# Five small constant TensorE products behind each piece of the state sums in a selective scan

## Time and profile before

| | us |
|---|---|
| median of 3 runs (5586.12 to 5604.31) | 5591.09 |
| profiled execution, its own time | 5583.17 |
| its span | 5581.4 |
| TensorE busy (products) | 4171.4 (75%) |
| VectorE busy | 3825.9 (69%) |
| ScalarE busy | 2731.3 (49%) |
| GpSimd busy | 1705.0 (31%) |

### The profile page before, as it was taken

How to read it: one execution, slowest core, us unless ns; L and a number is a source line. 1 busy time by engine, 2 the same in 40 slices (tenths; PEclk the granted TensorE clock), 3 DMA queues, 4 the chain that set the end, 5 groups by cost and what they waited for, 6 DMA issues and landing times. The chain is left out here.

```text
span 5581.4 us, 75326 instructions
## 1 busy us (share of the span) xinstructions
PE 4171.4 (75%) x23106; PEld 1512.8 (27%) x23106; DVE 3825.9 (69%) x5339; ACT 2731.3 (49%) x3579; POOL 1705.0 (31%) x938
## 2 busy tenths in 40 slices
PE   5587874632888886542787876676999999999994
PEld 3344441210111112210121112351333333333331
DVE  4355554455888884455789895556877877787783
ACT  1354550554444443465444444142666666666661
POOL 0000000144999991044799994000000000000000
PEclk8798996655667767755567678765999999999997
DMA  3311113123222222032222222132111111111114
GB/s 107 91 22 25 27 26 58 43 87 91 63 53 67 55 51 56 24 91 79 65 65 57 62 53 70 36 129 82 40 40 40 40 40 43 55 41 40 40 40 82
DMA packets 140635, 317.91 MB, mean 57 GB/s; under 512 B 27882, under 2 KB 86115, under 8 KB 135694
## 3 DMA queue, kind: packets, MB, share of 16 engines
q1 hardware_dynamic: 140238, 312.83, 20.9%
HBM read 204.28 MB, written 108.01 MB: 56 GB/s over the span
## 5 line engine op out<-in xcount | busy, mean ns | idle before, releaser
L1818 DVE TENSOR_REDUCE l3a_mx<-l3a_mx 128x1 f32<-128x384 f32 x2719 | 1326.0, 551 | 353.1 <-PE l3a_mx L1694 344.4
L1799 ACT ACTIVATE l3a_p<-l3a_s 128x1024 f32<-128x1024 f32 (+1 forms) x1080 | 978.4, 937 | 427.7 <-PE l3a_s L1715 416.6
L1252 POOL TENSOR_TENSOR l_scan_sc<-l_scan_s,l_scan_repc 128x768 f32<-128x768 f32 x576 | 1037.0, 1809 | 123.2 <-DVE l_scan_s L1230 114.2
L1694 PE MATMUL l3a_mx<-l3a_k,l3a_q 124*128 124x384 f16 x2719 | 867.7, 339 | 22.6 <-issue 18.7
L1189 ACT ACTIVATE l_scan_da<-l_scan_da,l_scan_a 128x768 f32<-128x768 f32 x576 | 504.1, 875 | 735.4 <-PE l_scan_da L1113 734.2
L1715 PE MATMUL l3a_s<-l3a_q,l3a_k 125*128 125x512 f16 (+1 forms) x2160 | 751.8, 362 | 29.1 <-issue 27.2
L1113 PE MATMUL l_scan_da<-l_scan_dt,l_scan_pick 96*128 96x512 bf16 (+1 forms) x1152 | 402.6, 444 | 259.2 <-DVE l_scan_s L1230 258.6
L1733 PE MATMUL l3a_o<-l3a_p,l3a_vh 128*32 128x512 f32 (+1 forms) x4332 | 592.6, 566 | 0.0
L1140 PE MATMUL l_scan_y<-l_scan_sc,l_scan_sum 128*32 128x256 f32 x3456 | 517.9, 540 | 0.8 <-POOL l_scan_sc L1252 0.7
L1113 PE MATMUL l_scan_dup<-l_scan_du,l_scan_pick 96*128 96x512 bf16 (+1 forms) x1152 | 384.1, 426 | 157.9 <-DMA l_scan_dt<-l_dtp 136.1
L1210 DVE TENSOR_TENSOR l_scan_bu<-l_scan_dup,l_scan_repb 128x768 f32<-128x768 f32 x384 | 363.0, 945 | 186.6 <-PE l_scan_dup L1113 161.9
(11 more groups left out here) (192 smaller groups left out, 5076.4 us busy)
## 6 DMA issues: line engine op xcount, KB each, us to landing
l3a_q<-l_qx SPq DMA_DIRECT2D x104, 486.0 KB
l_dup<-l_prep_parts_u SPq DMA_DIRECT2D x16, 1296.0 KB, 6.2
l_dtp<-l_prep_parts_t SPq DMA_DIRECT2D x16, 1296.0 KB, 8.3
l_scan_du<-l_dup SPq DMA_DIRECT2D x144, 144.0 KB
l_scan_dt<-l_dtp SPq DMA_DIRECT2D x144, 144.0 KB
l_scan_repb<-l_bcp SPq DMA_DIRECT2D x48, 384.0 KB
l_scan_repc<-l_bcp SPq DMA_DIRECT2D x48, 384.0 KB
l3a_q<-l_hx SPq DMA_DIRECT2D x104, 72.0 KB
```

The costliest lines, as they stand in the source:

```text
L1252: pool.tensor_tensor(SC[:, st % NSC, :], S[:, n, :], REPC[k % 2][:], ALU.mult).then_inc(weighted, 1)
L1694: pe.matmul(out[:, 0:RG], Q[h % HPB][0:rows, variant(g), qt * 128:(qt + 1) * 128], K[h % HPB][0:rows, g * RG:(g + 1) * RG], start=True, st ...
L1799: act.activation(P[:, g % NP, :, 0:w], s_ps[n % 2][:, :, 0:w], ACT.Exp).then_inc(exped, 1)
L1818: dve.tensor_reduce(MX[:, h % HPB, qt, g:g + 1], mx_ps[bank][:, 0:RG], AX_X, ALU.max)\
```

## The change

Behind each piece of the sums, TensorE also issues five products of constants: the weights are PICK's first 96 columns, the moving operand is 256 columns of PICK (bf16, 96 partitions), and the result goes to y_ps columns 768 to 1023, accumulated, and is never read. They are left out behind pieces 0 and 1 of a chunk's first triple and behind piece 2 of its last one, so behind three pieces in a row at each chunk's boundary. No wait is added and no other engine has a new instruction.

```diff
+                def keep_busy(tr, k):
+
+                    g = tr % NG
+                    if (g == 0 and k != NT - 1) or (g == NG - 1 and k == NT - 1):
+                        return
+                    for _ in range(5):
+                        pe.matmul(y_ps[:, TC:2 * CH], PICK[:, 0, 0:DI], PICK[:, 0:2, :].rearrange("p g q -> p (g q)"),
+                                  start=False, stop=False)
+
                 restore_du(GP)
                 for st in range(STEPS + LAG):
                     if st < STEPS:
@@ -1157,6 +1166,7 @@
                         restore(st, DT, da_ps[st % 2], dt_made)
                     if st >= LAG:
                         sum_piece((st - LAG) // NT, (st - LAG) % NT)
+                        keep_busy((st - LAG) // NT, (st - LAG) % NT)
```

## The result

| | before | after |
|---|---|---|
| median of 11 runs each, us | 5591.09 (5582.24 to 5606.84) | 5618.38 (5600.12 to 5627.18) |
| profiled execution, us | 5583.17 | 5624.51 |
| its span, us | 5581.4 | 5622.7 |
| mean granted TensorE clock | 0.791 | 0.842 |

What follows compares the result with a forecast made beforehand. The scans were taken as bound by TensorE's low clock, with all engines nearly full. Holding the clock saves 77 us, falls cost 24, so 53 us less: 5530 on the profiled execution, 5538 as median, range 5490 to 5600.

Steps and rivals of the forecast that it cites:

- The price of five: TensorE's queue in the scans: five added products with their weight loads take 0.57 us at full clock.
- the triple at full clock: Scans, VectorE: a triple with products behind piece 0 grows from 6.94 to 7.51 us, in three triples of four.
- the delay behind pieces 1 and 2: Scans: the dup there comes 0.57 us later but stays hidden; without that cover, up to 0.57 us each time.
- I estimate one in three chunks: Scans, bare steps at a chunk's boundary: the clock falls in one chunk of three; falls cost 24 us in all.
- I take 5 us of half clock behind a fall: Scans: each fall brings 5 us at half clock, costing 1.5 us.
- 0.29 us for each microsecond: Scans: price of half clock, from a covered triple taking 10.5 us for 7.5.
- the 77: Both scans: us saved with the clock held, 1.6 us a chunk over 24 chunks and 2 scans, before falls.
- rival 1: Chunk boundaries: bare steps lose the clock at every chunk, 72 of the 77 us lost, 5586, no change; chance 0.20.
- 29.5 + 0.5: Scans, us a chunk: 29.5 is VectorE's 4 x 6.94 + 3 x 0.57; falls cost 1.5 us in one chunk of three.
- the 35 us at full clock of before: Before's scan: a 35 us full-clock stretch holding several steps as thin as the bare ones, so falls aren't the rule.
- Layer 3 and all else unchanged: Outside the scans: the profile after should show no change in layer 3 or any other stage.
- Rival 3: Covered triples of the scans: products don't hold the clock; 211 us slower, 5802, with 60% at half clock; chance 0.10.

Runs made afterwards that it cites:

- moved_078: Against after with 32 filler instructions: the same 1080 products a scan, none behind piece 0, 7 behind piece 1, 8 behind piece 2; 5483.36 us, 0.9817 of before.
- moved_cover: As moved_078, with piece 1 of a chunk's first triple covered too (1248 products a scan); 5471.91 us, 0.9785 of before.
- cover11: Against after: five products also behind the two bare pieces at a chunk's start (11 pieces of 12), plus filler; 5571.67 us, 0.9970 of before.
- after_fill32: The kernel after with 32 semaphore increments more ahead of layer 3's loop, shift 4352; 5583.73 us, 0.9991 of before.
- only_behind_0: Against after: five products only behind piece 0 of triples 2 to 4, none elsewhere (360 a scan), plus filler; 5741.03 us, 1.0267 of before.
- moved_022: As moved_cover, but 2 products behind piece 1 and 2 behind piece 2 (336 a scan); 5473.29 us, 0.9801 of before.

## Why the prediction was wrong

Two steps failed; each by itself would have cost the forecast.

**What was right.** The price of five (0.57 forecast, 0.58 measured), the half-clock price (1.1, 1.09), the idle time ahead of L1220 (0.5, 0.55), the triple at full clock (7.51, 7.51) and at half clock (10.5, 10.09), and that the delay behind pieces 1 and 2 stays hidden: moved_078 has more behind them and is at GpSimd's bound. That the clock is what the scans lacked was right as well: with it, and nothing behind piece 0, a chunk takes 28.3 us for 31.1.

**"I estimate one in three chunks"** (the frequency of falls), and with it "I take 5 us of half clock behind a fall". The share of half clock in after's scans is 2 x 0.07 = 14% and 22%, so 4.3 us and 6.9 us of a mean chunk, where the forecast had 5 / 3 = 1.7. The trace's record of the granted clock shows both terms too small: 32 stretches at half clock in 46 chunks, each starting within 8 us of a chunk's start, 3.4 to 30.7 us long, 253 us together, 7.9 on average. At my own price of 0.29 us for each microsecond that is 73 us for 24, which takes back the 77. This is rival 1, but for 14 chunks that had no fall. In terms of a chunk:

| | us a chunk |
|---|---|
| before | 31.1 |
| clock held, nothing behind piece 0 (moved_cover) | 28.3 |
| three delays of 0.5 behind piece 0 | + 1.5 |
| half clock that is left, the rest | + 1.2 |
| after (means 30.58 and 31.34) | 31.0 |

The third row follows from cover11 and moved_cover, the fourth is what remains. I had 29.5 + 0.5. The reason that I gave for few falls, the 35 us at full clock of before, was the weak one: it was one stretch chosen because it was at full clock, and the share of full clock over the scan, 36%, spoke for rival 1. For the 5 us I had no row at all; the half-clock stretches of before's scans are 3.4 to 23.9 us long. The rival's 5586 is what after_fill32 measures (5583.73).

**"Layer 3 and all else unchanged."** Layer 3's attention took 31 us longer. The 7 second stalls are 23.3 us of it. Around each pair of stalls the clock was at half for 10.2 to 13.7 us, where before has 3.4 to 6.8 around its one, and over the stage TensorE's busy time is 1628.34 us for 1618.09 with the same 9494 products recorded: 10 us more. I had counted 4320 more instructions and priced them only where they run, not as code that moves all that stands behind them. This turned no change into slower, and no rival of mine had it. Rival 3, the clock not held, did not happen here: products of constants do hold the clock where they fill the right place. Behind piece 0 alone they do not (only_behind_0), which no rival of mine had in that form.

**What stays open.** At which place of the loop the second stall comes in, since three remainders were tried, and that the block's end is the reason; and why two products behind pieces 1 and 2 hold the clock when five behind piece 0 do not, as TensorE's busy share doesn't tell them apart: 560.27 of 660 us in only_behind_0's first scan, at a clock of 0.67, and 511.71 of 660 in moved_022's, at 0.90.

## What to carry to other kernels

Ask of each wait in a queue whether it has slack before filling it: here the same 1080 products a scan give nothing behind piece 0, 1 and 2 and 1.8% behind 1 and 2 alone, since the place behind piece 0 was the only one of the three on the path. When a stage is fully explained and the total doesn't add up, compare the untouched stages too: added code in an unrolled stage moves every later loop (here that cost 31 us), and a filler of a few dozen instructions tells that effect from the change itself. Estimate how often a thing happens from a whole stage, not from the stretch that shows it best.

## What the runs showed of the hardware beyond what was expected

- A loop of TensorE had one stall of 3.4 to 4.4 us a turn, or a second of 1.9 to 4.6 us, by its place in the instruction stream alone: 31 us in 7 turns, switched on by 224 instructions in before and off by 32 more in after. Each of these stalls ended 2.4 to 3.7 us behind the start of a 16384-byte instruction transfer, of which the profile counts one for each 256 TensorE instructions.
- Two small products of 256 columns behind pieces 1 and 2, 0.23 us of work each time, raised the granted clock of the scans from 0.68 and 0.72 to 0.90 and 0.93, with TensorE's busy share lower than before (511.71 of 660 us is 78%, for 84%).
- Products with weights of their own on the same rows of the array followed each other at 0.58 / 5 = 0.12 us each at full clock and 1.09 / 5 = 0.22 at half clock; their loads cost nothing visible.
